# A third buffer of softmax parts and a reordered step list in a two-layer graph attention kernel

## What is computed

```python
# layer 0, per graph
alpha = softmax(maximum(q @ k.T, 0) * (adj != 0), axis=1)      # q = x@wq, k = x@wk
x = layernorm(x + alpha @ (x @ weight))
# layer 1, per graph, 16 heads of 32
scores = where(adj == 0, -inf, (x@Wq+bq) @ (x@Wk+bk).T / sqrt(32))
x = layernorm(x + concat_heads(softmax(scores) @ (x@Wv+bv)) @ Wo + bo)
```

## Time and profile before

| | |
|---|---|
| median of 3 runs | 2856.49 us (2853.31 to 2862.83) |
| the profiled execution, its own time | 2860.47 us |
| its span, first to last instruction | 2858.6 us |
| mean granted TensorE clock | 0.953 of full |
| TensorE busy | 2594.3 us, 91% |
| VectorE / ScalarE / GpSimd busy | 2208.1 / 1965.3 / 818.9 us |
| share of the 16 DMA engines | 71.8% |

### The profile page before, as it was taken

One profiled execution on the slowest core, in us unless ns is written; L12 is line 12 of the kernel. 1 busy time (PEld: TensorE's weight loads), 2 busy tenths in 40 slices (PEclk: granted clock), 3 DMA queues, 4 the chain that ended last, 5 costly groups with the idle time before them and its releaser, 6 DMA issues.

```text
span 2858.6 us, 58570 instructions
## 1 busy us (share of the span) xinstructions
PE 2594.3 (91%) x20552; PEld 1391.8 (49%) x20552; DVE 2208.1 (77%) x4052; ACT 1965.3 (69%) x6286; POOL 818.9 (29%) x1416
## 2 busy tenths in 40 slices
PE   6899999999999989899999999999999999989985
PEld 3444555544555544455444545444545444445542
DVE  4478877778888778877778877778877778877786
ACT  3367766767767667766767767767766667766776
POOL 0123332123333123322223332223332233331232
PEclk9999999999999999999999999999999999999997
DMA  4487777877777777667787777787767776667765
GB/s 142 97 158 150 146 151 146 163 162 155 147 155 144 158 157 151 143 140 150 164 162 147 149 144 153 163 165 144 152 142 151 163 159 142 152 140 157 162 138 110
DMA packets 1059926, 426.77 MB, mean 149 GB/s; under 512 B 982192, under 2 KB 998576, under 8 KB 1059632
## 3 DMA queue, kind: packets, MB, share of 16 engines
q1 hardware_dynamic: 1059632, 423.03, 71.8%
HBM read 49.55 MB, written 33.55 MB: 29 GB/s over the span
## 4 chain that ended last, share of the span: by engine, by line
DVE 23%; SPq 17%; ACT 16%; POOL 12%; DMA 11%; PE 11%; issue 10%; ACTq 0%; DVEq 0%; POOLq 0%
SPq L321 12%; ACT e L525 7%; DMA pT<-p_p 7%; PE front L346 6%; DVE sm L646 4%; DVE p_p L546 4%; DMA adjT<-adj 3%; DVE bT L546 3%; PE fin_bank L346 3%; POOL ln L696 3%; SPq L326 3%; POOL ln L693 2%; POOL parts L702 2%; ACT y_sb L501 2%; DVE v_p L546 1%
## 5 line engine op out<-in xcount | busy, mean ns | idle before, releaser
L525 ACT ACTIVATE e<-sm,nmax 128x128 f32<-128x128 f32 x2048 | 790.1, 388 | 22.1 <-DVE nmax L650 21.4
L546 DVE SCALAR_TENSOR_TENSOR p_p<-e,p_p 128x512 f16<-128x512 f32 x512 | 392.3, 766 | 234.4 <-ACT p_p L533 233.8
L705 POOL TENSOR_TENSOR o_p<-o_sb,o_p 128x512 f16<-128x512 f32 x128 | 150.9, 1179 | 1474.1 <-ACT o_p L538 1474.1
L533 ACT ACTIVATE p_p<-e 128x512 f16<-128x512 f32 x512 | 319.7, 624 | 320.2 <-DMA pT<-p_p 314.5
L346 PE MATMUL fin_bank<-W_O,oT 128*128 128x512 f16 x1536 | 428.2, 438 | 12.4 <-DMA oT<-o_p 12.4
L525 ACT ACTIVATION_READ_ACCUMULATOR e<-sm,nmax 128x1 f32 x2048 | 385.2, 188 | 0.0
L650 DVE TENSOR_REDUCE nmax<-sm 128x4 f32<-128x512 f32 x512 | 351.3, 686 | 17.7
L346 PE MATMUL front<-xT,W_A 128*128 128x512 f16 x1536 | 346.7, 381 | 19.9 <-DMA xT<-parts 12.4
L346 PE MATMUL front<-yT,W_Q 128*128 128x512 f16 x1536 | 349.4, 381 | 9.4 <-DMA yT<-parts 9.4
L346 PE MATMUL front<-W,bT 128*128 128x512 f16 x1536 | 351.7, 379 | 2.9 <-DVE bT L546 2.9
L346 PE MATMUL front<-W_V,yT 128*128 128x512 f16 x1536 | 353.3, 379 | 0.0
(11 more groups left out here) (86 smaller groups left out, 3477.6 us busy)
## 6 DMA issues: line engine op xcount, KB each, us to landing
q_st<-qk SPq DMA_DIRECT2D x384, 128.0 KB, 2.5
k_st<-qk SPq DMA_DIRECT2D x384, 128.0 KB, 2.5
x_sb<-in_x SPq DMA_DIRECT2D x128, 256.0 KB, 3.5
out_x<-z_sb SPq DMA_DIRECT2D x128, 256.0 KB, 2.5
adj_i<-in_adj SPq DMA_DIRECT2D x32, 256.0 KB, 5.2
pT<-p_p SPq DMA_TRANSPOSE x512, 3.2
xT<-parts SPq DMA_TRANSPOSE x128, 2.8
yT<-parts SPq DMA_TRANSPOSE x128, 2.8
```

What stands on the lines that cost most here:

```text
L525: act.activation(e1[:, k % 2, h, :], sm[:, k % SM_BUFS, h, :], ACT.Exp, bias=nmax[:, k % SM_BUFS, h:h + 1], accum_out=esum[:, n % 2, head: ...
L533: act.activation(p_p[:, k % P_BUFS, HI, :], e1[:, k % 2, :, :].rearrange("p h m -> p (h m)"), ACT.Copy, scale=P1_SCALE).then_inc(phi_ready, 1)
L546: return dve.scalar_tensor_tensor(out=dst, in0=src, scalar=scale, in1=hi, op0=ALU.mult, op1=ALU.subtract)
L705: pool.tensor_tensor(o_p[:, LO, :], o_sb[:, :], o_p[:, HI, :], ALU.subtract).then_inc(olo_ready, 1)
```

## The change

Four edits. P_BUFS becomes 3, and the index of the buffer (also that of sm and nmax, where it changes nothing) is now the running number of the step over all groups, since 16 is no multiple of 3; P k on ScalarE so waits for the transpose of P k-3. The space of adj_i is given up: the integers are loaded into e0, the layer 0 exponentials, read there by adj01 and then overwritten by alpha; the load has one more wait, for p0 of the group before. VectorE's step o has one more wait, for its own o of the graph before. And PASS is another order of the same 165 entries, with a few ages moved with them.

```diff
-P_BUFS = 2
+P_BUFS = 3
 PASS = [
...
 ]
...
-        adj_i = sb("adj_i", [P, GB, P], I32)
...
         e0 = sb("e0", [P, GB, P])
+        adj_i = e0[:, :, :].bitcast(I32)
...
                     wait(sp, adj01_ready, g)
+                    wait(sp, p0_ready, count(g, GB, 0))
                     sp.dma_start(adj_i[:, :, :], adj_d[g]).then_inc(adj_loaded, 16)
...
-                                           p_p[:, k % P_BUFS, :, :].rearrange("p a m -> p (a m)")).then_inc(pT_turned[k % PT_BUFS], 16)
+                                           p_p[:, count(g, STEPS, k) % P_BUFS, :, :].rearrange("p a m -> p (a m)")).then_inc(pT_turned[k % PT_BUFS], 16)
...
                 elif what == "o":
                     dve.wait_ge(exp_done, count(g, 4 * STEPS, HEADS * (k + 1)))
+                    wait(dve, o_ready, count(g, GB, k))
                     dve.reciprocal(einv[:, :], esum[:, k % 2, :]).then_inc(einv_ready, 1)
```

More of the change, by code:

```diff
@@ L59 @@
 PASS = [
-    ("xT", 1, 0), ("P", 10, 2), ("exp", 11, 2), ("pT", 11, 2), ("o", 1, 2), ("x_parts", 1, 0), ("P", 11, 2), ("PV", 6, 2),
-    ("o_parts", 1, 2), ("q", 2, 1), ("PV", 7, 2), ("xT", 2, 0), ("x_parts", 2, 0), ("q", 3, 1), ("oT", 1, 2), ("xT", 3, 0),
-    ("S", 14, 2), ("stack_q", 0, 1), ("exp", 12, 2), ("P", 12, 2), ("exp", 13, 2), ("x_parts", 3, 0), ("stack_q", 1, 1),
[18 rows of a table removed]
-    ("exp", 10, 1), ("x_parts", 0, -1),
[12 rows of a table added]
+    ("exp", 8, 1), ("stack_q", 2, 0), ("pT", 12, 1), ("P", 8, 1), ("exp", 9, 1), ("stack_q", 3, 0), ("exp", 10, 1),
+    ("fin", 0, 1), ("S", 12, 1), ("P", 9, 1), ("S", 13, 1), ("q", 0, 0), ("P", 10, 1), ("PV", 6, 1), ("stack_k", 0, 0),
+    ("x_parts", 0, -1), ("o", 1, 1), ("x_parts", 1, -1), ("q", 1, 0), ("x_parts", 2, -1), ("exp", 11, 1), ("adjT", 0, -1),
+    ("P", 11, 1), ("stack_k", 1, 0), ("q", 2, 0), ("PV", 7, 1), ("q", 3, 0), ("stack_k", 2, 0), ("S", 14, 1),
+    ("x_parts", 3, -1), ("exp", 12, 1), ("o_parts", 1, 1), ("PV", 8, 1), ("stack_k", 3, 0), ("pT", 13, 1), ("S", 15, 1),
[5 rows of a table added]
 ]
@@ L524, in step @@
                         head = 4 * quad + h
-                        act.activation(e1[:, k % 2, h, :], sm[:, k % SM_BUFS, h, :], ACT.Exp,
-                                       bias=nmax[:, k % SM_BUFS, h:h + 1],
+                        act.activation(e1[:, k % 2, h, :], sm[:, count(g, STEPS, k) % SM_BUFS, h, :], ACT.Exp,
+                                       bias=nmax[:, count(g, STEPS, k) % SM_BUFS, h:h + 1],
                                        accum_out=esum[:, n % 2, head:head + 1]).then_inc(exp_done, 1)
@@ L532, in step @@
                         act.wait_ge(pT_turned[n % PT_BUFS], 16 * (n // PT_BUFS + 1))
-                    act.activation(p_p[:, k % P_BUFS, HI, :], e1[:, k % 2, :, :].rearrange("p h m -> p (h m)"),
+                    act.activation(p_p[:, count(g, STEPS, k) % P_BUFS, HI, :], e1[:, k % 2, :, :].rearrange("p h m -> p (h m)"),
                                    ACT.Copy, scale=P1_SCALE).then_inc(phi_ready, 1)
@@ L645, in step @@
                     wait(dve, exp_done, count(g, 4 * STEPS, 4 * (k + 1 - SM_BUFS)))
-                    dve.scalar_tensor_tensor(out=sm[:, k % SM_BUFS, :, :], in0=s_bank[k % 2][:, :].rearrange("p (h m) -> p h m", h=4),
+                    dve.scalar_tensor_tensor(out=sm[:, count(g, STEPS, k) % SM_BUFS, :, :], in0=s_bank[k % 2][:, :].rearrange("p (h m) -> p h m", h=4),
                                              scalar=SCORE_UNSCALE, in1=maskb[:, n, :].unsqueeze(1).to_broadcast([P, 4, P]),
@@ L649, in step @@
                     dve.wait_ge(sm_ready, count(g, STEPS, k + 1))
-                    dve.tensor_reduce(nmax[:, k % SM_BUFS, :], sm[:, k % SM_BUFS, :, :], AX_X, ALU.max, negate=True).then_inc(nmax_ready, 1)
+                    dve.tensor_reduce(nmax[:, count(g, STEPS, k) % SM_BUFS, :], sm[:, count(g, STEPS, k) % SM_BUFS, :, :], AX_X, ALU.max, negate=True).then_inc(nmax_ready, 1)
                 elif what == "P":
                     dve.wait_ge(phi_ready, count(g, STEPS, k + 1))
-                    lo_part(p_p[:, k % P_BUFS, LO, :], e1[:, k % 2, :, :].rearrange("p h m -> p (h m)"), P1_SCALE,
-                            p_p[:, k % P_BUFS, HI, :]).then_inc(plo_ready, 1)
+                    lo_part(p_p[:, count(g, STEPS, k) % P_BUFS, LO, :], e1[:, k % 2, :, :].rearrange("p h m -> p (h m)"), P1_SCALE,
+                            p_p[:, count(g, STEPS, k) % P_BUFS, HI, :]).then_inc(plo_ready, 1)
                 elif what == "o":
                     dve.wait_ge(exp_done, count(g, 4 * STEPS, HEADS * (k + 1)))
+                    wait(dve, o_ready, count(g, GB, k))
                     dve.reciprocal(einv[:, :], esum[:, k % 2, :]).then_inc(einv_ready, 1)
```

## The result

The changed kernel takes **2742.15 us** (median of 4 runs, 2739.27 to 2742.94), beside 2858.99 us (2853.31 to 2862.83) for the kernel before in the same series: ratio 0.9591 [0.9572, 0.961], 117 us faster. The profiled execution took 2742.14 us, its span is 2740.3 us.

A forecast was written before the change was run, and what follows sets the result against it. VectorE was taken to pace the part from z 0 to q 0, TensorE the rest. Terms -1.1 + 0.7 - 1.4 = -1.8 us a pass, -56 us over 31 passes, gave 2801 us, range 2750 to 2866.

The forecast's parts named there:

- Third buffer: ScalarE's P waits for pT: removing them frees idle time mostly beside the path, worth 0 to 0.1 us a pass.
- stretch II: Part of a pass from first q matmul to next z 0, 45.51 us in the pass read; forecast 44.4 after.
- adjT earlier: End of the pass: adjT issued 4.2 us earlier removes z 0's wait for p0, -1.1 us a pass.
- stretch I: Part of a pass from first z matmul to q 0, 39.64 us, VectorE setting the pace; forecast 38.9 after.
- Stretch I up to g 3: VectorE from z 0 to g 3: its changed list takes 28.0 us against 27.36, +0.7 us a pass.
- From g 3 to q 0: Between VectorE's g 3 and first q matmul: 10.9 us against 12.28, slow clock kept for fin 0, -1.4 a pass.
- The count of passes: Whole kernel: the gain per pass was multiplied by 31 steady passes, with 0 for first layer and drain.
- Moved DMAs and waits: SyncE's reordered transposes and loads have time enough; the wait in o costs 0 to 0.1 us, twice a pass.
- Hidden anyway: P wait and adjT never on the path, VectorE's extra S eats the rest: about 2850 us; chance 0.14.
- The clock holds or yT decides: fin 0 at full clock, q 0 comes with yT: 1.5 us less a pass, 2754 us; chance 0.16.
- The collision of GpSimd and VectorE: More P low parts stretched by GpSimd: pass +1.2 us if all six are hit, 2894 us; chance 0.12.
- The slow clock reaches q: All 12 q matmuls at half speed: net +0.8 us a pass, 2881 us; chance 0.08.

The follow-up runs named there:

- e1: Kernel before, old order, with only the third P buffer and its space added: 2809.73 us, ratio 0.9809.
- e4: Kernel before, old order and two buffers, with only adjT issued earlier, behind stack_k 0: 2816.63 us, ratio 0.9832.
- e3: Changed kernel with adjT issued late again, after stack_k 2, nothing else: 2742.05 us, ratio 0.9575.
- e7: Kernel before, old order, with both the third buffer and adjT after stack_k 0: 2758.45 us, ratio 0.9637.
- e6: Kernel before, old order, with third buffer, adjT after stack_k 0 and both o_parts moved: 2756.18 us, ratio 0.9621.
- e5: Kernel before, old order and two buffers, with only o_parts 3 moved behind exp 2 and o_parts 0 behind g 2: 2892.24 us, ratio 1.0101.
- v3: Changed kernel with v 1 moved into TensorE's gap behind S 8, yT 1 behind oT 0, fin 1 behind p0: 2736.61 us, ratio 0.9568; repeated 2739.49 us.

## Why the prediction was wrong, by its own steps

**The step that failed first: *Third buffer*, "Directly on the path it is worth 0 to the 0.1 us a pass".** e1 measured 53 us, 1.57 us a pass. The bound was taken from one pass of the kernel before, in which TensorE worked 44.46 of 45.51 us of stretch II and lost the rest at z 0 alone. With the mean stretch II of 46.73 us, the same subtraction gives 2.3 to 2.4 us to be won there, and z 0's wait explains only about 1 us of it. With that alone put right, the sum would have been -2.4 - 0.7 = -3.1 a pass, -96 us, about 2760 us, inside the range. The comparison of 314.5 us of P waits with 34.3 of TensorE's compared the wrong things: when the P waits went in e1, z 0's wait stayed, and what went on TensorE were small idle times before PV, t and alpha. The one pass that I read had almost none of them.

***adjT earlier*, -1.1.** Right in mechanism on the old order: its wait and z 0's are gone, and the list's place for it does that alone (e4). The size was 1.43 us a pass alone, since half of it came in stretch I. In the new order the three stack DMAs that I counted are not needed, since all of SyncE's queue runs earlier (e3): either would do. The division in this term was off too: 34.3 by 30 is 1.14, and without the 4.5 us of the first wait it is 1.03.

***Stretch I up to g 3*, +0.7.** This term was mis-sized as well. Over all 29 steady passes VectorE's g 3 starts 27.38 us behind z 0 before and 27.21 after: -0.2. VectorE had its work done sooner than forecast, because the 1.5 us of stretched P low which I carried over are not there. Part of that came back, since VectorE then stands for TensorE's g 3: 16.7 us in all over the span, 0.86 in the pass shown, in which g 3 starts 27.69 us behind z 0 (320.86 less 293.17):

```profile
320.86 0.69 DVE L627 SCALAR_TENSOR_TENSOR y_sb<-front,x_sb 128x512 f32<-128x512 f32 x1 [0.86 <-PE front L347]
```

***From g 3 to q 0*, -1.4.** Over all passes 11.92 us became 10.60: -1.3, as forecast. The pass shown has 330.74 - 320.86 = 9.88 us against 12.28, which is -2.40, another reading that one pass gets wrong. In it the walk to S 11 was right (forecast 4.86, measured 4.92), and fin 0 to q 0 took 4.73 us where I kept 5.89. In the mean that last part went from 5.54 to 5.01. The slow clock stayed, as forecast: fin 0 takes over 3 us in all 29 passes of both kernels, and TensorE is at the lower level for 6.36 us a pass in both. But the slow fin 0 is a little shorter, 4.70 us in the mean against 4.90, so 0.2 us of the gain lie there.

Together stretch I gave 1.51 us where the two terms gave 0.7. On the old order the early adjT brings 0.76 of it (e4), the buffer 0.25 (e1), both 0.89 (e7).

***The count of passes*, 31.** There are 29 steady ones. The filling and draining passes gave some 5 us, for which I took 0, so this changes little.

***Moved DMAs and waits*, and fin 1 ahead of alpha, 0.** Right for the path: TensorE has no new wait before PV or t, and the wait in o does not show (o's first instruction starts 0.60 us after the one ahead of it, 318.44 less 317.84, as before, 305.87 less 305.27). Off the path there is a new wait: ScalarE's x_parts stands 76.6 us in all, 30 times, for the load of x, 0.4 us before.

**The signs.** Of those I named, right: adjT's wait gone, stretch II 44.4 (mean 44.35), P waits under 100 us, fin 0 over 4, mean P low under 800 ns, sm waits under 160. Wrong: stretch I 38.9 (mean 37.80).

**The rivals.** *Hidden anyway* is refuted by e1 and e4, each over 45 us alone. *The clock holds or yT decides* gave 2754 us, near the measured time, but its mechanism did not occur: fin 0 is slow in every pass, and q waits for yT only once in the whole span. That the number fits is luck. *The collision of GpSimd and VectorE* went the other way: in the pass shown no P low is stretched. Before, two a pass were, 9.8 and 26.0 us after z 0, each begun about 0.3 us behind an o_parts of GpSimd; over the whole span 59 of the 512 take over 1 us before and 2 after. That agrees with the rule of the Trainium skill (SBUF: State Buffer, Who interferes with whom), and the order came out on its good side. Yet e6 against e7 shows that moving the collisions away was worth nothing measurable on the old list, where yT took its place. *The slow clock reaches q* did not occur.

## What to carry to other kernels

Before a gain is bounded by one pass, take the mean of each stretch over all passes: the difference between a stretch and the bounding engine's own work in it is what can be won, whatever the named waits sum to. Where every engine works through its list in order, a wait on an engine off the path is not harmless just because the bounding engine waits little for that very instruction; ask what stands behind it in its queue, and whether the bounding engine's idle time is spread over many small waits. And an order and its buffers are one design: adjT's place was worth 46 us in one order and none in the other, and the new order with one buffer less is 7% slower than the kernel before.

## What the runs showed of the hardware beyond that

A P low on VectorE took 1.36 us in the kernel before where GpSimd's subtraction had begun 0.34 us earlier, against 0.68 undisturbed; the two timelines:

```profile
309.87 1.36 DVE L546 SCALAR_TENSOR_TENSOR p_p<-e,p_p 128x512 f16<-128x512 f32 x1
```

```profile
309.53 1.16 POOL L705 TENSOR_TENSOR o_p<-o_sb,o_p 128x512 f16<-128x512 f32 x1 [6.53 <-ACT o_p L538]
```

What I had not expected is that moving both such pairs apart (e5) takes 0.08 us off the mean of 512 P low, 42 us of busy time on the engine that is busiest in stretch I, and that the time shows none of it, neither there nor between e7 and e6. Nor that v3, with a mean clock of 0.976 in place of 0.951 and 2.35 us a pass at the lower level in place of 6.36, ends at the same time: what the clock gave back, the new waits of PV 4 and alpha took.
